# Rounded upper parts of the keys: issued from ScalarE's DMA queue behind the copy that makes them, in place of SyncE's queue

## What is computed

```
K = jnp.einsum('bpd,ihd->biph', x, W_K)
Q = jnp.einsum('bpd,ihd->biph', x, W_Q)
V = jnp.einsum('bpd,ihd->biph', x, W_V)
scores = jnp.einsum('biph,biqh->biqp', K, Q)      # masked, divided by sqrt(64)
attn = jax.nn.softmax(...)
z = jnp.einsum('biph,biqp->biqh', V, attn)
```

## Time and profile before

| | us |
|---|---|
| median of three runs | 2050.61 |
| lowest and highest of the three | 2047.91, 2051.98 |
| span of the profiled execution | 2046.9 |
| ScalarE busy in that span | 965.0 (47%) |
| TensorE busy in that span | 1884.8 (92%) |
| share of TensorE in the chain that ended last | 58% |
| upper-part DMAs (L1780) issued by SyncE | 84 |

### The profile page before, as it was taken

How to read it: one execution, slowest core, us unless ns; L and a number is a source line. 1 busy time by engine, 2 the same in 40 slices (tenths; PEclk the granted TensorE clock), 3 DMA queues, 4 the chain that set the end, 5 groups by cost and what they waited for, 6 DMA issues and landing times.

```text
span 2046.9 us, 31623 instructions
## 1 busy us (share of the span) xinstructions
PE 1884.8 (92%) x9864; PEld 1249.3 (61%) x9864; DVE 1387.3 (68%) x3825; ACT 965.0 (47%) x2008; POOL 1232.5 (60%) x1600
## 2 busy tenths in 40 slices
PE   5899999999996899999999999998889999888985
PEld 4555556656596566666666567887456565445554
DVE  8887777787444767666666456455778888776733
ACT  2435444454464555555555435544444544444443
POOL 1668976767745457777777800012457767788744
PEclk8999999999998999999999999999999999999997
DMA  5335132131162433443443220001212222223133
GB/s 146 95 88 151 53 72 53 42 83 41 29 197 78 102 90 82 112 93 81 107 98 86 59 86 22 1 12 33 74 47 55 68 68 64 78 55 84 44 109 102
DMA packets 125967, 155.56 MB, mean 76 GB/s; under 512 B 21880, under 2 KB 66200, under 8 KB 125544
## 3 DMA queue, kind: packets, MB, share of 16 engines
q1 hardware_dynamic: 121704, 145.42, 28.6%
q0 software_dynamic: 4096, 8.12, 1.2%
HBM read 47.84 MB, written 17.40 MB: 32 GB/s over the span
## 4 chain that ended last, share of the span: by engine, by line
PE 58%; POOL 12%; DVE 12%; issue 10%; ACT 4%; DMA 2%; SPq 1%; POOLq 0%; DVEq 0%; ACTq 0%
PE P L867 57%; POOL acc L1644 5%; POOL yd L1661 3%; DVE P L2035 2%; POOL pr L1622 2%; POOL xg L1652 1%; POOL acc L1641 1%; ACT pr L1403 1%; DVE mx L2024 1%; DVE mx L2045 1%; DMA qA<-hq 1%; PE P L963 1%; DVE qB L1996 1%; DMA xg<-xs,sidx 0%; DVE bst L1936 0%
## 5 line engine op out<-in xcount | busy, mean ns | idle before, releaser
L1644 POOL TENSOR_TENSOR acc<-acc,pr 128x512 f32<-128x512 f32 (+3 forms) x768 | 677.1, 904 | 61.1 <-ACT pr L1403 36.7
L1403 ACT ACTIVATE pr<-P 128x512 f32<-128x512 f32 (+1 forms) x768 | 395.9, 567 | 308.9 <-PE P L867 307.2
L867 PE MATMUL P<-pr,vt 128*64 128x512 f32 (+3 forms) x2304 | 431.0, 499 | 17.7 <-POOL pr L1622 17.5
L867 PE MATMUL P<-qA,kA 128*128 128x512 f32 (+2 forms) x1024 | 395.8, 390 | 27.1 <-ACT pr L1403 22.2
L1622 POOL TENSOR_SCALAR_AFFINE_SELECT pr<-pr 128x256 f32<-128x256 f32 x384 | 157.0, 409 | 357.0 <-ACT pr L1403 249.5
L867 PE MATMUL P<-qB,kB 128*128 128x512 f32 (+2 forms) x1024 | 368.1, 365 | 0.0
L867 PE MATMUL P<-kA,qA 128*128 128x512 f32 (+2 forms) x1152 | 310.5, 371 | 21.3 <-DVE rd L2083 5.9
L867 PEld LDWEIGHTS P<-qA,kA 128*128 128x128 f32 x1024 | 194.6, 190 | 152.3 <-issue 72.5
L2024 DVE TENSOR_REDUCE mx<-P 128x1 f32<-128x512 f32 x384 | 244.6, 683 | 56.1 <-PE P L867 54.5
L867 PEld LDWEIGHTS P<-pr,vt 128*64 128x64 f32 x2304 | 141.5, 137 | 221.2 <-issue 148.6
L867 PEld LDWEIGHTS P<-kA,qA 128*128 128x128 f32 x1152 | 192.0, 194 | 128.1 <-issue 68.1
(11 more groups left out here) (350 smaller groups left out, 2717.2 us busy)
## 6 DMA issues: line engine op xcount, KB each, us to landing
qA<-hq SPq DMA_DIRECT2D x384, 128.0 KB
kA<-stage SPq DMA_DIRECT2D x158, 128.0 KB
qB<-qB SPq DMA_DIRECT2D x96, 128.0 KB, 2.4
kB<-stage SPq DMA_DIRECT2D x79, 128.0 KB
nr<-null_share SPq DMA_DIRECT2D x64, 128.0 KB, 2.9
yd<-in_c_zero SPq DMA_DIRECT2D x32, 128.0 KB, 2.8
w<-in_L_W SPq DMA_DIRECT2D x16, 256.0 KB, 5.0
xg<-xg SPq DMA_DIRECT2D x24, 129.0 KB
```

The costliest lines, as they stand in the source:

```text
L867: return P.matmul(out, lhs, rhs, start=start, stop=stop)
L1403: S.activation(a.pr[slot][:, r, 512 - wide:512], m.bank[b][:, 512 - wide:512], AF.Exp, scale=0.125).then_inc(s.free[b], 1)
L1644: G.tensor_tensor(acc[:, sl], acc[:, sl], pt[:, sl], ALU.add).then_inc(s.acc, 1)
```

## The change

The upper-part DMAs move from SyncE's program into ScalarE's, right behind the copy L1361. ScalarE waits there for the scores that last used the key slots, then for its own copy (`k_hi`), and issues one DMA for each head. SyncE does nothing for `khi` any more; the wait for `k_hi` that stood at its `khi` item is now ahead of the `kB` DMAs. Destination, sizes and semaphores of the DMAs are as before.

```diff
@@ scalar_program @@
                 S.copy(pl.key_stage(m, *k)[0][0:wide, :].bitcast(FR), src[0:wide, :]).then_inc(s.k_hi, 1)
+                for h in pl.key_heads(L, kp):
+                    if pl.k_before(L, bb, h):
+                        w.wait_ge(*pl.filled(*pl.k_before(L, bb, h)))
+                w.wait_ge(s.k_hi, n)
+                for r, h in enumerate(pl.key_heads(L, kp)):
+                    S.dma_start(a.kA[0:64, pl.heads[L, bb, h][0], c * 512:c * 512 + 512],
+                                pl.key_stage(m, *k)[0][64 * r:64 * r + 64, :]).then_inc(s.keys_a[pl.second_keys(*k)], 16)
@@ sync_program @@
-            elif kind in ("khi", "klo", "kb"):
+            elif kind in ("klo", "kb"):
                 L, bb, kp, c = k
                 a, cs, second = m.A[L], slice(c * 512, c * 512 + 512), pl.second_keys(*k)
                 heads = [(pl.heads[L, bb, h][0], slice(64 * r, 64 * r + 64)) for r, h in enumerate(pl.key_heads(L, kp))]
                 for h in pl.key_heads(L, kp):
                     if pl.k_before(L, bb, h):
                         w.wait_ge(*pl.filled(*pl.k_before(L, bb, h)))
-                if kind == "khi":
-                    w.wait_ge(s.k_hi, od.nth(*item))
-                    for slot, rows in heads:
-                        Y.dma_start(a.kA[0:64, slot, cs], pl.key_stage(m, *k)[0][rows, :]).then_inc(s.keys_a[second], 16)
-                elif kind == "klo":
+                if kind == "klo":
                     w.wait_ge(*pl.emptied("k", *k))
                     for slot, rows in heads:
                         Y.dma_start(a.kA[64:128, slot, cs], pl.key_stage(m, *k)[1][rows, :]).then_inc(s.keys_a[second], 16)
                 else:
+                    w.wait_ge(s.k_hi, od.nth("khi", *k))
                     for slot, rows in heads:
                         Y.dma_start(a.kB[64:128, slot, cs], pl.key_stage(m, *k)[0][rows, :]).then_inc(s.keys_b[second], 16)
```

## The result

| | before | after |
|---|---|---|
| median of the first comparison (four runs each), us | 2050.33 | 2062.14 |
| lowest and highest, us | 2047.91, 2051.98 | 2060.98, 2063.89 |
| ratio, 95% interval | | 1.0073 (1.0061 to 1.0085) |
| span of the profiled execution, us | 2046.9 | 2062.1 |
| same two kernels in two later comparisons, medians | 2052.85; 2051.28 | 2064.02; 2062.75 |

The changed kernel is slower by 0.7%, 11.8 us; two repetitions beside other kernels gave 11.2 and 11.5 us between the medians (ratios 1.0058, 1.0037 to 1.0079, and 1.0051, 1.0034 to 1.0067). The two profiles differ by 15.2 us, more than the medians: the first profile of before was a short one.

A forecast was written before the change was run, and what follows sets the result against it. TensorE's own work was taken as the bound, so any new wait in its stream counts; 3.2 + 2.0 + 0 + 1.1 + 0.3 + 0.8 = 7.4 us gave a 2054.3 us span, 2058 us median, range 2048 to 2072.

The forecast's parts named there:

- The hold: Behind the copy, two issues hold ScalarE: its next exponential starts 1.3 us after the copy's end, a 1.4 us shift.
- (a): ScalarE is held longer than SyncE was, 0.25 us more an issue: 13 us more, 2071 us; chance 0.15.
- (b): ScalarE's hold is short or hidden, deciding below some 0.5 us an item: 2050 us, no change; chance 0.18.
- First halves in layer 1: Late row maxima delay SyncE's DMAs and the lower key parts TensorE needs: 3.2 us plus 2.0 us.
- the five even jobs: Five layer 1 jobs (first-half copies ending 787.5 to 1092.7, without 1032.2): delay 1.03, slack 0.60, 0.43 us each, 2.2 together.
- the sixth: Layer 1 job where TensorE already stands idle 0.69 us before the key load: all 1.03 us goes through.
- the odd jobs: Seven layer 1 jobs between the six others: keys landing late in two of seven, 2.0 us, bounds 0 and 7.2.
- Second halves in layer 1: Exponentials behind the copy free the score banks just in time, margins 0.15 and 0.07 us, at sixteen places: 0 us.
- In layer 3: Four items of one DMA each, in places where ScalarE or SyncE waits anyway: 0 us.
- The starts: Start of layer 0: value weights' copy behind the issues, 1.1 us; start of layer 1: 2.3 less 1.52, 0.8 us.
- rival (c): SyncE's queue was the bound; TensorE's waits for query DMAs, some 4 us, are gained: 2046 us, faster; chance 0.06.
- Rival (d): Slack is larger than the rows say, only the 3.2 us are left: 2054 us, edge of no change; chance 0.12.

The follow-up runs named there:

- the kernel with 62 issues: ScalarE issues 62 of the 84 DMAs, only where nobody waits behind them, SyncE the rest; 2048.98 us beside 2049.32 for the kernel before, ratio 1.0001.
- the second profile of before: The kernel before, unedited, run and profiled once more: 2051.89 us, span 2050.1 us.
- The third DMA: The changed kernel plus a third DMA issued by ScalarE behind the two in layer 1, from the third key item on: 2080.82 us, ratio 1.0163.
- the repetition: The changed kernel run once more with no edit: 2064.02 us, ratio 1.0058 to the kernel before.
- second halves only: Against the kernel before, ScalarE issues the upper parts of second key halves alone, SyncE those of first halves: 2060.21 us beside 2052.85, ratio 1.0033.

## Why the prediction was right, and where its sum fell short

**The direction and the mechanism held.** I had said slower at 0.68, 2058 us with a range to 2072; 2062.14 lies in it. The number is 4 us short, and the stretches say which terms did that.

**The hold.** I took 1.3 us from the copy's end to the next exponential, out of SyncE's 1.12 for two issues. It is 1.27 at all but two of the 27 steady key items of layer 1 that have an exponential next. This was the term with the widest bounds, and the nearest row gave it to 0.03 us. Rivals (a) and (b) needed another hold: (a) 0.5 us more per item, (b) under 0.5 us in all. Neither is there as a rule. (a) rested on a mutual hold of the two issuing engines at second halves, or on slower issues. At second halves ScalarE's pair takes the same 1.12 us as at first halves, though SyncE's lower parts begin at +0.75, while ScalarE's second issue is under way. Where both issue from the start, at first halves of the kernel with 62 issues, it takes 1.12 us too in 11 of 15 places. The other half of (a) did come, in a few places: of the slow issues of the earlier trace rows, which I had left out for the median, two or three of 1.3 to 1.8 us fall to ScalarE in the steady part of layer 1 in each profile of the change, and the jobs with them grew by 1.0, 1.0 and 1.6 us.

**First halves in layer 1, 5.2 us.** The steady stretch lost 6.2, so the term was right in size, but in part by luck. At the five even jobs I had a delay of 1.03 less a slack of 0.60, 0.43 each. The keys came 1.12 us later, not 1.03, and the weight load moved by 0.60 to 0.62 at four of them and 0.72 at the last: by the counts of the semaphore `keys_a` the last share was there 0.58 us before the load, and the load can't follow closer than 0.06, which makes the slack 0.52 (0.42 at the last). TensorE makes up 0.1 to 0.2 us of it right behind: from one copy to the next these jobs grew by 0.48 to 0.49 us, 2.4 in sum in place of 2.2. At the sixth (copy ending at 1032.22 before) I let all 1.03 through, since TensorE already stood idle for 0.69 us. That was wrong: the load came 8.73 us after the copy before and 8.68 after, and the second profile of before had 0.23 us of idle time there. The keys were late there in both profiles of before, but not by a chain that simply shifts with ScalarE. At the odd jobs I took two of seven and 2.0 us for keys that land late. In the first profile after the loads of four of seven moved by 0.4 to 0.9 us and these jobs grew by 1.7 us, but 1.0 of that is in the two jobs with a long issue of ScalarE, which is another cause. And about 0.7 us each went where my sum had nothing: to the routing step at 750 us, and to the steady second halves together.

**Second halves in layer 1, 0 us.** Nearly right for the steady jobs: in the first profile each of the twelve from 775 to 1109 us lengthened the way to the next copy by 0.04 to 0.07 us, 0.65 in sum. The third DMA showed that the margin was as thin as stated: 0.53 us of load delay for 0.65 us more of hold. But the working spoke of the two exponentials behind the copy as if they stood there in all sixteen jobs. In the first job the copy of x stands there too. This is the place before, ScalarE, VectorE and TensorE:

```profile
705.03 0.59 ACT L1361 CAST stage<-P 128x512 fp32r<-128x512 f32 x1 [0.45 <-PE P L867]
705.51 0.59 ACT L1319 CAST xh<-P 128x512 fp32r<-128x512 f32 x1
...
706.14 0.69 DVE L1968 TENSOR_TENSOR xl<-P,xh 128x512 fp32r<-128x512 f32 x1 [0.75 <-ACT xh L1319]
706.75 0.68 DVE L2005 TENSOR_TENSOR stage<-P,stage 128x512 fp32r<-128x512 f32 x1
...
707.57 1.08 PE L867 MATMUL P<-acc,ones 128*64 128x512 f32 x4 [0.77 <-DVE stage L2005]
```

And after:

```profile
711.07 1.12 ACTq L1367 DMA_DIRECT2D kA<-stage  x2
712.23 0.58 ACT L1319 CAST xh<-P 128x512 fp32r<-128x512 f32 x1 [1.19 <-issue]
...
712.84 0.69 DVE L1972 TENSOR_TENSOR xl<-P,xh 128x512 fp32r<-128x512 f32 x1 [2.03 <-ACT xh L1319]
...
714.28 1.43 PE L867 MATMUL P<-acc,ones 128*64 128x512 f32 x4 [2.03 <-DVE stage L2009]
```

TensorE, VectorE and ScalarE form a chain without slack, and 0.77 us of idle time became 2.03: 1.3 us. A step of the routing (`pn`) stands behind the next copy in the same way. In layer 3 I had written "in places where ScalarE or SyncE waits anyway", without looking at who waits for ScalarE. At the second of its places the exponential starts 0.66 us after the copy's end behind one DMA, where it had started 0.11 before it; the chain behind is later by that, and TensorE's wait for a later exponential went from 0.45 to 1.10:

```profile
1707.14 0.50 PE L867 MATMUL P<-qA,kA 128*128 128x512 f32 x1 [1.10 <-ACT pr L1410]
```

So the step that fell short is this one: the cost of a second half was read at one steady job and set to nothing for all 18 of layers 1 and 3; at four of them it was 0.7 to 1.3 us. Run by themselves these four cost 3.5 us (0.6 to 6.4), close to the 4 us by which the forecast was short.

**The starts.** 1.1 and 0.8 us were said. At layer 0 the loss is 1.03 us in every profile of the change; at layer 1 the mean of 0.9 is no more than two profiles of before differ by. At layer 0 the value weights' copy stands behind the issues as foreseen: TensorE's wait of the earlier trace rows grew from 1.38 to 2.41. At layer 1 the first wait of the earlier trace rows grew from 1.10 to 1.58 and the second, for the queries (1.52), is gone.

```profile
677.66 0.74 PE L867 MATMUL P<-kA,qA 128*128 128x512 f32 x2 [1.58 <-ACT vt L1375]
...
678.94 0.62 PE L867 MATMUL P<-kA,qA 128*128 128x512 f32 x2
```

This is the gain that rival (c) lived on, and it is real: in the first profile TensorE gained 1.5 us there. But between 660 and 672 us (times of before) it had lost 2.2 us, close to the 2.3 that I gave the delays of ScalarE. Rival (d), a larger slack, fell at the even jobs.

## What to carry to other kernels

A DMA issue is not free for the engine that makes it: here 0.5 to 0.6 us each, 1.38 us of shift for two with the wait on its own copy, and all that stands behind on this engine pays. Before moving an issue to a compute engine, list what follows it there at every place, not at a typical one; the same two DMAs cost almost nothing, 0.5 or 1.3 us by what stood behind them. Count the slow issues too, not the median alone: in layer 1 they cost nothing on SyncE, and three of them on ScalarE cost 1.6 us in one execution. If they must go, put them where the engine idles next: with 62 of 84 moved so, the time was that of the kernel before.

## What was unexpected in the hardware

**The clock after an idle time.** At the first second half of layer 1 TensorE was idle for 2.03 us in the first profile after and in the repetition. In the first profile the granted clock then fell (0.65 and 0.79 of 2.4 GHz in the next two stretches of 3 us), and 128x384 matmuls took 0.53 us:

```profile
711.00:714.00 3.00, 1.25 (x6) 0.68 (x4) 1.16 (x2) 1.61 (x4) 1.26 (x2) 1.00 0.39 87
714.00:717.00 3.00, 2.72 (x8) 1.40 (x9) 1.85 (x4) 1.22 (x2) 2.78 (x3) 0.65 0.54 121
717.00:720.00 3.00, 3.00 (x12) 1.20 (x10) 2.75 (x5) 0.99 (x3) 1.18 (x2) 0.79 0.27 59
```

In the repetition, with the same idle time, it stayed at 1.00 and they took 0.34:

```profile
715.00:718.00 3.00, 1.34 (x6) 0.75 (x4) 1.06 (x2) 1.71 (x4) 1.25 (x2) 1.00 0.39 87
718.00:721.00 3.00, 2.63 (x12) 1.45 (x14) 2.50 (x5) 1.48 (x3) 2.89 (x3) 1.00 0.49 114
```

(Columns as in the earlier trace rows; the clock is the third number from the end.) The stretch 705 to 735 lost 2.77 us with the fall and 1.28 without. Of the seven profiles with 2.0 to 2.1 us of idle time at this place, with and without DMAs from ScalarE, the clock fell behind it in three (the change twice, second halves only) and stayed in four. The same program at the same place can pay twice the wait, or once.

**Two issuing engines at once.** They hardly hold each other up: ScalarE's pair of DMAs took 1.12 us in 11 of 15 places where SyncE began to issue within 0.04 us of it, as it does alone, and SyncE's four 2.5 to 2.7 us against 2.40.

**Long issues.** Of the 168 issues of key parts in the first profile of before 13 took over 0.8 us, up to 1.67, where the usual ones take 0.46 to 0.6. In layer 1 they come back at the same first halves (copies ending at 756.9, 940.4 and 1063.3): in both profiles of before all three have one, on SyncE, and in the three of the change two, two and three, on ScalarE. The cause was not tested.
